# A patch tokenizer, attention and channel-mix block for 64 images: one hand-written periodic order against a place and a PSUM bank for every single operation

## The reference, cut to what matters

```python
# x (64, 3, 224, 224), txt (64, 77, 256)
t = patches of 16 x 16 x 3              # (64, 196, 768)
t = layernorm(t) @ W + b                # (64, 196, 256)
h = concat([layernorm(t), txt], 1)      # (64, 273, 256)
# "attention": n, s = 64, 273; q, k, v are (n, 16 heads, s, 16)
scores = einsum('nqhd,nkhd->nhqk', Q, K) / 4   # as (n, h, s, d): the softmax runs over 16 rows of ONE token,
attn = softmax(scores)                          # so each token has a 16 x 16 table of its own
out = einsum('nhql,nlhd->nqhd', attn, V).reshape(n, s, e)
h = h + out @ Wo.T + bo
# channel mix, with the token before (zero at the first token of an image) as x_prev
z = layernorm(h); xr, xk = mixes of z and x_prev
h = h + sigmoid(xr @ Wr.T) * (square(relu(xk @ Wk.T)) @ Wv.T)
```

## Time and profile before

| | before |
|---|---|
| median of 3 runs | 1819.36 us (1818.13 to 1831.14) |
| profiled execution: its own time, its span | 1823.79 us, 1822.1 us |
| mean granted TensorE clock | 0.912 of full |
| PE, PEld busy | 1468.3 us (81%), 1369.7 us (75%) |
| DVE, ACT, POOL busy | 1232.8 (68%), 1122.8 (62%), 910.0 us (50%) |
| DMA queue of SP | 676,780 packets, 222.28 MB, 65.8% of 16 engines' span |

### The profile page before, as it was taken

The page is one execution under the profiler, slowest core; times in us unless marked ns, Lnnn a source line. Parts: engine busy times, 40 slices in busy tenths (PEclk is TensorE's granted clock), DMA queues, the critical chain, the costliest instruction groups (busy, mean ns, idle before and its releaser), DMA issues. The chain is left out here.

```text
span 1822.1 us, 51616 instructions
## 1 busy us (share of the span) xinstructions
PE 1468.3 (81%) x17678; PEld 1369.7 (75%) x17678; DVE 1232.8 (68%) x3109; ACT 1122.8 (62%) x2410; POOL 910.0 (50%) x1593
## 2 busy tenths in 40 slices
PE   4577888888879877988787888898888887886866
PEld 3576787787878767877777777787778787876766
DVE  4576777676867666867666777686777776765543
ACT  3445666666757665766565666676666766754643
POOL 2131455555645554556444555465545644555547
PEclk8687999999989988999898999999999998988988
DMA  5268767766777676777666667776877786656650
GB/s 119 52 132 127 123 143 128 124 132 125 151 122 139 139 131 118 122 142 143 126 111 113 135 119 149 128 147 139 131 119 139 154 126 118 138 104 118 109 90 27
DMA packets 677038, 225.57 MB, mean 124 GB/s; under 512 B 591853, under 2 KB 647980, under 8 KB 676780
## 3 DMA queue, kind: packets, MB, share of 16 engines
q1 hardware_dynamic: 676780, 222.28, 65.8%
HBM read 119.28 MB, written 90.05 MB: 115 GB/s over the span
## 5 line engine op out<-in xcount | busy, mean ns | idle before, releaser
L998 PE MATMUL bank<-wqkv,xnT 128*128 128x384 f32 x1656 | 337.0, 347 | 2.0 <-ACT dT L979 1.6
L998 PEld LDWEIGHTS bank<-wqkv,xnT 128*128 128x128 f32 x1656 | 285.0, 192 | 7.1 <-issue 2.8
L1102 PE MATMUL bank<-wtok,xT 128*126 128x258 f32 (+1 forms) x1800 | 253.4, 297 | 0.0
L637 POOL TENSOR_TENSOR mixp<-mixf,mixp 128x384 fp32r<-128x384 f32 x184 | 184.8, 1012 | 101.2 <-ACT mixp L974 100.6
L1102 PEld LDWEIGHTS bank<-wtok,xT 128*126 128x126 f32 (+1 forms) x1800 | 234.9, 198 | 0.0
L895 ACT ACTIVATE arena<-qk,ymask 128x384 f32<-128x384 f32 x368 | 196.9, 610 | 44.1 <-PE bank L1051 39.8
L1127 PE MATMUL bank<-ident,on 128*128 128x128 f32 x276 | 61.2, 379 | 195.5 <-DMA on<-o_dram 193.3
L1127 PEld LDWEIGHTS bank<-ident,on 128*128 128x128 f32 x276 | 44.4, 193 | 204.7 <-DMA on<-o_dram 203.8
L642 POOL TENSOR_TENSOR dT<-dT 128x384 f32<-128x384 f32 x92 | 76.1, 827 | 224.3 <-ACT dT L979 223.9
L950 ACT ACTIVATE onT<-bank 128x384 fp32r<-128x384 f32 x92 | 44.0, 490 | 221.9 <-PE bank L1127 217.6
L823 DVE TENSOR_TENSOR onT<-bank,onT 128x384 fp32r<-128x384 f32 x92 | 50.1, 556 | 187.2 <-ACT onT L950 184.8
(11 more groups left out here) (119 smaller groups left out, 3510.7 us busy)
## 6 DMA issues: line engine op xcount, KB each, us to landing
qkv_dram<-qkvt SPq DMA_DIRECT2D x138, 384.0 KB, 3.3
xim<-in_x SPq DMA_DIRECT2D x128, 294.0 KB
qk<-qkv_dram SPq DMA_DIRECT2D x46, 768.0 KB, 8.4
arena<-qkv_dram SPq DMA_DIRECT2D x368, 48.0 KB
out<-h SPq DMA_DIRECT2D x136, 128.0 KB, 2.8
o_dram<-probs SPq DMA_DIRECT2D x304, 48.0 KB, 1.8
on<-o_dram SPq DMA_DIRECT2D x73, 128.0 KB
hc<-in_txt SPq DMA_DIRECT2D x24, 77.0 KB
```

The source lines that it names most:

```text
L637: mix_lo.done(P.tensor_tensor(mixp[:, w, 1, kk, :], mixf[:, kk, :], mixp[:, w, 0, kk, :].bitcast(F32), ALU.subtract))
L998: ins = mm(psum, left(a, k), right(b, k), start=t == 0, stop=t == len(terms) - 1)
L1102: ins = mm(place("tok", 0, t)[0:pr, 0:E + 2], xT[:, a, ch, :, :].rearrange("p i w -> p (i w)")[:, r0:r0 + pr], wtok[:, b, ch, :], start=n ...
```

## The change

`AT` becomes a table of every operation's own place (8,572 places, one operation each), and `BANK` one of every operation's own bank (any of the eight for every kind). The two orders hold the same operations; only qk_in changes its engine. The layout of two buffers, the cutting of the transfers and the issuing engine of one change too:

- `spread` cuts a transfer whose row count divides badly over 16 engines into a multiple of 16 and a rest; used for the patch rows, the text rows and the rows of `o_in`.
- `pt2` holds its columns as (q, r) in place of (r, q), so that the two halves of a result lie in neighbouring partitions; `o_out` then stores two runs of 48 tokens with one transfer where neither is cut by an image edge. `o_dram` gets a stride `OSTEP` for each image.
- `out` of a full chunk is one transfer behind the last tile in place of three.
- `qk_in` is issued by ACT, which waits for `qkv_out` to have landed and for the last readers of `qk`.

```diff
-SLOT = 5376
-AT = dict(load=[0], xcols=[2623, 3093, 3346], sq=[5465], ...
-BANK = dict(x=[5, 0, 5], tok=[7, 2], xt=[3, 4], ...
+AT = dict(
+    load=[
+        [5, 14, 28, 54, 93, 139, 185, 259, 389, 439, 535, ...
+BANK = dict(
+    x=[
+        [int(b) for b in "2552321142213645101050552147526356413126772342246166511631265562"],
...
+WHEN = {step: (kind, j, k) for kind, rows in AT.items() for j, row in enumerate(rows) for k, step in enumerate(row)}
+STEPS = sorted(WHEN)
...
+def spread(a, rows, most):
+    engines = max(n for n in range(1, 17) if rows % n == 0)
+    whole = rows // 16 * 16
+    return [(a, rows)] if rows <= most * engines else [(a, whole), (a + whole, rows - whole)]
...
 def row_pieces(c):
-    return [(lo // T, lo % T, hi - lo) + place_of(lo)[1:] for lo, hi in cut(CT * c, min(CT * c + CT, TOKENS), [TT, T])]
+    return [(at // T, at % T, rows) + place_of(at)[1:]
+            for lo, hi in cut(CT * c, min(CT * c + CT, TOKENS), [TT, T]) for at, rows in spread(lo, hi - lo, 9)]
...
 def head_pieces(c):
+    for j in range(4):
+        runs = [CT * c + RUN * j, CT * c + RUN * (4 + j)]
+        runs = [first for first in runs if first < TOKENS]
+        whole = all(first % T + RUN <= T for first in runs)
+        if len(runs) == 2 and whole and runs[0] // T % OIMAGES <= runs[1] // T % OIMAGES:
+            out.append((runs[0], RUN, 32 * j, 2, 0))
+        else:
+            for r, first in enumerate(runs):
                 for lo, hi in cut(first, first + RUN, [T]):
+                    out.append((lo, hi - lo, 32 * j + r, 1, lo - first))
...
+OUT_DMAS = [1 if rows == CT else -(-rows // TT) for rows in OUT_ROWS]
...
-        pt2 = sb("pt2", [128, BLK, 2, 2, HD])
+        pt2 = sb("pt2", [128, BLK, 2, HD, 2])
...
+        SPARE = [0, 1, 3, 4, 6]
...
-                for k in due(s, "qk_in", 0):
-                    after_all(qkv_out, k)
...
+                for k in due(s, "qk_in", 0):
+                    qkv_out.wait(act, k)
+                    settle(act)
+                    if k > 0:
+                        kb_sb.wait(act, k - 1, 4 * PARTS)
+                        settle(act)
+                        q_sb.wait(act, k - 1, 2 * PARTS)
+                        settle(act)
+                    src = qkv_dram[k % SLOTS, :, :, 0:2 * HD]
+                    qk_in.done(act.dma_start(qk[:, :, :], src.rearrange("(g t) i j -> (t i) g j", t=8)))
...
-                            pt_sb.done(A.activation(pt2[64 * rr:64 * rr + 64, PB * part:PB * part + PB, :, rr, :],
+                            pt_sb.done(A.activation(pt2[64 * rr:64 * rr + 64, PB * part:PB * part + PB, :, :, rr],
```

More of the change, by code:

```diff
@@ L76 @@
-STEPS = sorted({a + PERIOD[kind] * k for kind, at in AT.items() for a in at for k in range(COUNT[kind])})
+AT = dict(
+    load=[
[4 rows of a table added]
+    ],
+    xcols=[
[12 rows of a table added]
+    ],
+    sq=[
[4 rows of a table added]
+    ],
+    ssq=[
[4 rows of a table added]
+    ],
+    sqm=[
[6 rows of a table added]
+    ],
+    x=[
[12 rows of a table added]
+    ],
+    xh=[
[12 rows of a table added]
+    ],
+    xl=[
[12 rows of a table added]
+    ],
+    tok=[
[6 rows of a table added]
+    ],
+    statc=[
[6 rows of a table added]
+    ],
+    statr=[
[6 rows of a table added]
+    ],
+    rstd1=[
[6 rows of a table added]
+    ],
+    txt=[
[4 rows of a table added]
+    ],
+    yn=[
[6 rows of a table added]
+    ],
+    st2=[
[6 rows of a table added]
+    ],
+    mv2=[
[6 rows of a table added]
+    ],
+    rstd2=[
[6 rows of a table added]
+    ],
+    hg=[
[6 rows of a table added]
+    ],
+    h=[
[6 rows of a table added]
+    ],
+    hdma=[
[6 rows of a table added]
+    ],
+    st3=[
[9 rows of a table added]
+    ],
+    mv3=[
[9 rows of a table added]
+    ],
+    rstd3=[
[3 rows of a table added]
+    ],
+    xn=[
[9 rows of a table added]
+    ],
+    xt=[
[6 rows of a table added]
+    ],
+    xnh=[
[6 rows of a table added]
+    ],
+    xnl=[
[6 rows of a table added]
+    ],
+    hb=[
[3 rows of a table added]
+    ],
+    qkv=[
[18 rows of a table added]
+    ],
+    qb=[
[18 rows of a table added]
+    ],
+    qkv_out=[
[9 rows of a table added]
+    ],
+    qk_in=[
[3 rows of a table added]
+    ],
+    v_in=[
[3 rows of a table added]
+    ],
+    qplace=[
[12 rows of a table added]
+    ],
+    kspread=[
[24 rows of a table added]
+    ],
+    s=[
[6 rows of a table added]
+    ],
+    mx=[
[6 rows of a table added]
+    ],
+    sub=[
[6 rows of a table added]
+    ],
+    exp=[
[6 rows of a table added]
+    ],
+    pt=[
[6 rows of a table added]
+    ],
+    ptc=[
[12 rows of a table added]
+    ],
+    av=[
[6 rows of a table added]
+    ],
+    rec=[
[6 rows of a table added]
+    ],
+    osb=[
[6 rows of a table added]
+    ],
+    o_out=[
[3 rows of a table added]
+    ],
+    o_in=[
[3 rows of a table added]
+    ],
+    ont=[
[6 rows of a table added]
+    ],
+    onh=[
[6 rows of a table added]
+    ],
+    onl=[
[6 rows of a table added]
+    ],
+    wo=[
[9 rows of a table added]
+    ],
+    h2=[
[9 rows of a table added]
+    ],
+    st4=[
[9 rows of a table added]
+    ],
+    mv4=[
[9 rows of a table added]
+    ],
+    rstd4=[
[3 rows of a table added]
+    ],
+    z=[
[9 rows of a table added]
+    ],
+    zt=[
[6 rows of a table added]
+    ],
+    carry=[
[3 rows of a table added]
+    ],
+    ztc=[
[6 rows of a table added]
+    ],
+    d=[
[6 rows of a table added]
+    ],
+    edge=[
[3 rows of a table added]
+    ],
+    mix=[
[12 rows of a table added]
+    ],
+    mixh=[
[12 rows of a table added]
+    ],
+    mixl=[
[12 rows of a table added]
+    ],
+    k=[
[6 rows of a table added]
+    ],
+    kr=[
[6 rows of a table added]
+    ],
+    ksq=[
[6 rows of a table added]
+    ],
+    kah=[
[6 rows of a table added]
+    ],
+    kal=[
[6 rows of a table added]
+    ],
+    r=[
[9 rows of a table added]
+    ],
+    rt=[
[9 rows of a table added]
+    ],
+    val=[
[9 rows of a table added]
+    ],
+    rv=[
[9 rows of a table added]
+    ],
+    add=[
[9 rows of a table added]
+    ],
+    out=[
[9 rows of a table added]
+    ],
+)
```

127 lines of the change are left out of this document (96 added, 31 removed), and 550 rows, old and new, of tables (add, av, carry, d).

## The result

| | before | after |
|---|---|---|
| median | 1818.74 us (4 runs) | 1721.42 us (4 runs, 1706.33 to 1723.43) |
| ratio to before, 95% interval | | 0.944 (0.9365 to 0.9516) |
| profiled execution: its own time, its span | 1823.79, 1822.1 us | 1719.71, 1718.0 us |
| PE busy, PE idle (span less busy) | 1468.3, 353.8 us | 1442.6, 275.4 us |
| waits of `ont` for `o_dram` | 193.3 us | 103.0 us |

The change makes the kernel 5.6% faster. I had forecast 1604 us with a range of 1520 to 1710: the direction is right, the gain is about half of the one forecast, and the time lies just outside the range.

The account below looks back on a forecast made before the run. TensorE set the pace, losing 193.3 us to `ont` waiting for `o_in`'s rows. Span 1822.1 - 193.3 + 40 - 55, less 7 at the ends, gave 1607, hence a 1604 us median; range 1520 to 1710.

Parts of the forecast that it names:

- What bounds the kernel: TensorE sets the pace; its largest idle loss, 193.3 us, is `ont` waiting for `o_in`'s rows, which also lowers the clock.
- The split: Splitting `o_in`'s rows cuts landing from 4.5 to 2.3 us for 0.5 us more issuing, net 1.7 us off the chain.
- Own places: New order puts 15.5 us of TensorE work over the chain to `ont`, leaving 40 us of its 193.3 us of waits.
- the two counts: Shortfalls of cover to `ont`: 23 us counted from the last `av`, 41 us from `o_in`; overlapping, so 40 us taken.
- The clock: TensorE's granted clock between 300 and 1600 us rises from 0.93 to 0.97, worth about 55 us over the run.
- The other waits: TensorE's small waits, 65 us in the middle stretch, move both ways; sum kept, with 40 us either way.
- `qk_in` on ACT: ACT's wait for `qkv_out` costs TensorE nothing, 24 us if cover is gone; SP no longer stands behind `qk_in`.
- Paired stores: `o_out` falls from 9.2 to 6.9 transfers a chunk, worth +1.0 to -0.8 us a chunk; +1.0 taken.
- Landings stay slow: Rival: rows of `o_in` still land slowly, from more small pieces or denser traffic; 1694 us, chance 0.16.
- The order does not fit the chip: Rival: a static order without slack loses in many small TensorE waits, 4 us more a chunk; 1788 us, chance 0.05.
- ACT and SP block each other: Rival: SP still stands 6 to 7 us, ACT waits for `qkv_out`; 1964 us with half reaching TensorE, chance 0.06.

Follow-up runs that it names:

- b_split: The kernel before plus `spread` in its three lists of pieces, nothing else; 1702.7 us, ratio 0.9328.
- a_sp_early: The changed kernel with `o_out` placed straight behind its `osb` and `o_in` straight behind the `o_out` and `zt` it waits for; 1755.3 us, ratio 0.9634.
- a_qk_late: The changed kernel where, in 13 chunks, ACT issues `qk_in` only after the rows of the nearby `o_in` have landed; 1753.5 us.
- a_two_q: The changed kernel with every second transfer of `o_out` issued by ACT; 1758.7 us, ratio 0.9634.
- b_split_two_q: The kernel before plus split pieces, with every second store of `o_out` issued by ACT; 1646.25 us, ratio 0.9023.
- b_split_two_q_in: The kernel before plus split pieces, with every second `o_out` store and every second `o_in` piece issued by ACT; 1686.9 us, ratio 0.9228.
- b_all_transfers: The kernel before's places and banks with every change of the transfers, `qk_in` on ACT too; 1863.3 us, ratio 1.0206.
- The pair of cuts: `qk_in` cut to an eighth of its bytes from the second chunk on (wrong results): changed kernel 1593.5 us, kernel before with split pieces 1675.2 us.
- a_small_qk: The changed kernel with `qk_in` bringing only an eighth of its bytes from the second chunk on (wrong results); 1593.5 us, ratio 0.8736.
- a_qk_sp: The changed kernel with only `qk_in` given back to SP at the same places; 1739.8 us, ratio 0.9538.
- b_transfers: The kernel before's places and banks with the changed transfers and layouts, `qk_in` still issued by SP; 1724.8 us, ratio 0.9452.
- a_unpair: The changed kernel with every run of `o_out` a store of its own, the changed layout kept; 1763.8 us, ratio 0.9669.
- the third and fourth sets: Later follow-up runs moving issue places or engines, cutting `qk_in`, or separating pairs from single `out`, on either order; complete kernels took 1646.25 to 1863.3 us.

## Why the prediction was wrong in its size

**What bounds the kernel: right.** `ont` waiting for its rows was the largest loss, it cost in the clock too, and its size went with how the rows divide. b_split, an edit of that division alone, takes 121 us off. One reading was wrong on the way: the granted clock is at 8 or 9 tenths in 38 of the 40 slices, not in half of them. Nothing was worked out from it.

**The split: right in mechanism, too small in its place.** Landing 4.5 to 2.3 us was the forecast, 4.6 to 2.0 was measured in b_split. I took it as one term of a chain that the own places would cover anyway. In the old order it alone gives as much as the whole change.

**Own places: this is the step that failed.** I counted 15.5 us of TensorE work between the last `av` of chunk k + 1 and `ont` of chunk k for 11.0 before, and set it against a chain of 12.8 us, measured and corrected in the old order. The chain is no constant of the kernel. In the changed kernel, over the 33 chunks whose `ont` waits for rows, it takes 18.6 us; in b_split, over 39 such chunks, 12.9. The cover itself came as counted: 18.6 less some 3 us of wait is 15.5. It was the need that had grown by 5.8 us. Piece by piece (means, b_split and changed kernel): from `av` to the first store 2.0 and 3.5, the stores' issue 4.5 and 4.7, from there to `o_in` 2.0 and 4.7, its issue 2.5 and 2.5, the landing 1.9 and 3.2. The new order issues `o_out` and `o_in` later in SP's line, with other transfers between (in 12 chunks `v_in`, whose issue takes up to 12.5 us), and meets `qk_in` with the landing. My own count of the second distance, 3.8 us from `o_in` to `ont` against 4.4 needed, said as much; I let the two counts overlap and took 40 us. At the measured 3.2 us of landing it would have said 5.3.

That is what one reads; what it costs is another matter, for a_sp_early, a_qk_late and a_two_q all mended the chain (35.7, 62.3 and 44.7 us of waits) and all ran 32 to 37 us slower. TensorE's other idle time grew from 172 us to 268, 234 and 266, more than the waits shrank. In the old order b_split_two_q won 55 us of waits and 56 us of time, but not one for one: its span fell by 62 us, 55 of waits and 18 of busy time less 11 more of other idle time. Nor does every us of that wait count there: b_split_two_q_in took 29 us more off it and ran 41 us slower, and b_all_transfers 50 us and ran 139 slower, because ACT stood. The pair of cuts (128 us in the changed kernel, 27 in the old order) shows what the changed kernel runs short of: the time of `qk_in`'s 6144 small packets a chunk. That its chains are all laid out with equally little to spare, so that what is taken from one is asked of the next, is my reading of these numbers; no run tests it.

**The clock: too high.** I took 0.97 for the middle; it is 0.94 between 300 and 1600 us, since long waits (up to 8.2 us) stayed. Of 55 us 26 came. Where the waits did go, the clock came: 0.951 in a_small_qk, 0.953 in b_split_two_q.

**The other waits.** I kept them at 160 us; they are 172, within the 40 us. b_split, in the old order, has 171.

**`qk_in` on ACT.** That SP would be free of the standstill behind it is half right. The longest issue of a patch store was 7457 ns and is 1681 (L1229 after):

```profile
L1229 SPq DMA_DIRECT2D hc<-yh x282: 508/769/1681, 50.0 to 1568.4; - x141
```

But `v_in`, which follows `qkv_out` as `qk_in` does, takes 366 us of SP in all for 343 in a_qk_sp and 306 before, and where it stands ahead of `o_out` it holds up the chain. By the medians the move is worth 18 us in the new order, where the intervals overlap a little, and it costs 139 in the old one, whose cover I had rightly counted as 0.0. What I did not count is the other side of it. In the old order, on SP's queue, `qk_in` comes behind `o_in`; here, on ACT's, it can come in between. Its own landing grows to 10.5 us, from 8.4 before and 8.2 in a_qk_sp; in the old order, too, it is 10.5 on ACT (b_all_transfers) for 7.7 on SP (b_transfers):

```profile
qk<-qkv_dram ACTq DMA_DIRECT2D x46, 768.0 KB, 10.5
```

The Trainium skill's page DMA: Bandwidth & Descriptors (section Issuing engines are not separate DMA queues) says that transfers of all issuing engines share the same 16 DMA engines. The trace agrees: rows on SP's queue wait for ACT's transfer, 6.3 us in the chunk shown. Its other half, that only issue time is saved, holds as well, but I had read too little into it: all issues of SP together take 1086 us for 1165 in a_qk_sp, 80 us less, of which the issues of `qk_in` themselves are 21.

**Paired stores: half right.** A pair takes a median of 0.59 us to issue for 0.42 of a single store before, so a chunk's stores take 4.7 us for 4.5. The "+1.0" that I took of +1.0 to -0.8 is not there. But the pair is not what costs: 108 of the 316 stores are pairs, and the 208 that stay single take 0.59 us as well, in the old order too (b_transfers), as all 424 do in a_unpair (6.2 us a chunk). The changed layout made every store slower to issue, and against such single stores the pairing is worth 42 us in the new order. I had priced the pair and not the layout.

**The rivals.** "Landings stay slow" gave 1694 us, is nearest to what happened, and is right in part: landings stayed slow (4.2 to 6.9 us) in 9 of the 13 chunks above, through a collision, and not through the traffic at large. "The order does not fit the chip" resembles what the third and fourth sets found, but it put the loss in small waits, which are no larger in sum than b_split's. ACT waiting for `qkv_out` costs 139 us in b_all_transfers, near the 150 that "ACT and SP block each other" took for half of its waits, but little in the change itself, where no line of ACT waits for it for more than 7 us in all.

**Left open.** The bank table was not tried by itself, nor the split of `o_in` without that of the patch and text rows, nor the new order with `v_in` behind `o_out`. Of the changed kernel's 172 us of other idle time 154 are still there in a_small_qk, so most of it does not hang on `qk_in`; which chains are behind it is open.

## What to carry to other kernels

Look first at how the rows of a transfer divide over the 16 DMA engines: splitting off a multiple of 16 gave 6.7% here, with one small function and the order as it was. Cover counted in one order must not be set against a chain measured in another, for the order also decides when the chain's transfers are issued and what lands beside them. And the largest wait in the table is a place to look, not a price. Here five edits made that wait shorter and the run slower, three in the new order and two in the old one, each time with other waits grown by more; so read TensorE's whole idle time after such an edit, not the one wait.
